# Softmax row sums: from ones-matmuls and a trip through DRAM to accumulating exponentials, with the score matmuls issued twice

## The reference

```python
def _L0_attn_ref(x, gamma, Wq, Wkv, Wo):      # 16 heads of 64, one shared key/value head
    xn = layer_norm(x, gamma)
    q = xn @ Wq
    k, v = jnp.split(kv_input @ Wkv, 2, axis=-1)
    sim = jnp.einsum('bhid,bjd->bhij', q * SCALE, k)
    sim = jnp.where(j_idx > i_idx, neg, sim)
    attn = jax.nn.softmax(sim, axis=-1)
    out = jnp.einsum('bhij,bjd->bhid', attn, v)
    return out @ Wo
def _L0_ffn_ref(x, W_fc, W_proj):
    h = jnp.square(jax.nn.relu(x @ W_fc.T))
    y = h @ W_proj.T
    ...                                        # five threshold steps on y
    return jnp.sum(spks, axis=0) / NUM_STEPS
x = x + 0.5 * _L0_ffn_ref(_layernorm(x), W_fc, W_proj)
x = x + _L0_attn_ref(_layernorm(x), gamma, Wq, Wkv, Wo)
x = x + 0.5 * _L0_ffn_ref(_layernorm(x), W_fc, W_proj)
```

## Time and profile before

| | us |
|---|---|
| median of 3 runs | 2724.68 |
| lowest and highest run | 2653.78, 2790.25 |
| the profiled execution | 2656.24 |
| its span, slowest core (core 3) | 2654.7 |
| spans of the 8 cores | 2634.5 to 2654.7 |
| mean granted TensorE clock of the cores | 0.799 to 0.812 |

### The profile page before, as it was taken

One profiled execution on the slowest core, in us unless ns is written; L12 is line 12 of the kernel. 1 busy time (PEld: TensorE's weight loads), 2 busy tenths in 40 slices (PEclk: granted clock), 3 DMA queues, 4 the chain that ended last, 5 costly groups with the idle time before them and its releaser, 6 DMA issues.

```text
span 2654.7 us, 20937 instructions; the slowest of 8 cores (2634.5 to 2654.7 us)
## 1 busy us (share of the span) xinstructions
PE 1732.8 (65%) x6660; PEld 619.3 (23%) x6660; DVE 876.8 (33%) x1482; ACT 560.6 (21%) x1004; POOL 109.0 (4%) x207
## 2 busy tenths in 40 slices
PE   0396599998355535344556655565664869999993
PEld 0042244443011101011111111111111324444441
DVE  0420364462454443232211121111112432536345
ACT  0320111030200022222323433234240221202010
POOL 1001000002200000000000000000001000000000
PEclk9897899999689655666677676676767979999997
DMA  9509312203610121322334334434435102231322
GB/s 218 107 32 232 101 56 80 96 33 103 95 23 14 15 48 32 72 48 55 64 72 75 60 73 80 77 64 79 87 64 152 70 17 77 74 131 55 132 72 80
DMA packets 320380, 206.86 MB, mean 78 GB/s; under 512 B 289914, under 2 KB 294074, under 8 KB 307986
## 3 DMA queue, kind: packets, MB, share of 16 engines
q1 hardware_dynamic: 293442, 104.22, 18.6%
q0 software_dynamic: 25680, 92.92, 13.3%
q10 hardware_dynamic: 1152, 8.39, 1.0%
HBM read 125.82 MB, written 25.38 MB: 57 GB/s over the span
## 4 chain that ended last, share of the span: by engine, by line
PE 52%; DMA 18%; DVE 14%; ACT 6%; issue 5%; another core or an unknown queue 3%; DVEq 1%; POOL 0%; SPq 0%; ACTq 0%; POOLq 0%
PE pb L469 15%; PE pb L415 12%; PE pb L683 9%; DMA WB<-WB 8%; PE pb L690 8%; ACT WB L787 5%; DVE acc L363 4%; DMA sums_d<-acc 3%; PE pb L568 2%; PE pb L829 2%; DMA Q<-wprojT 2%; DVE acc L704 2%; DVE WB L731 2%; DMA WB<-sums_d 1%
## 5 line engine op out<-in xcount | busy, mean ns | idle before, releaser
L415 PE MATMUL pb<-Q,WB 128*128 128x512 bf16 x2048 | 457.1, 384 | 73.2 <-DVE Q L391 50.3
L787 ACT ACTIVATE WB<-pb,ncb 128x512 bf16<-128x512 f32 (+3 forms) x640 | 342.9, 650 | 715.5 <-PE pb L767 415.3
L469 PE MATMUL pb<-HB,Q 128*128 128x512 bf16 x2048 | 449.9, 382 | 47.7 <-DMA Q<-wprojT 32.6
L421 ACT ACTIVATE Q<-pb 128x512 bf16<-128x512 f32 x256 | 152.8, 597 | 747.4 <-PE pb L415 662.2
L762 PE MATMUL pb<-WB,Q 64*128 64x512 bf16 (+3 forms) x320 | 145.6, 477 | 249.1 <-ACT WB L787 249.0
L683 PE MATMUL pb<-WB 128*64 128x512 bf16 x544 | 262.3, 482 | 68.7 <-DMA WB<-WB 66.4
L415 PEld LDWEIGHTS pb<-Q,WB 128*128 128x128 bf16 x2048 | 199.2, 98 | 329.9 <-issue 101.6
L469 PEld LDWEIGHTS pb<-HB,Q 128*128 128x128 bf16 x2048 | 200.5, 98 | 297.1 <-issue 62.4
L690 PE MATMUL pb<-WB,ones 128*1 128x512 bf16 x544 | 241.1, 443 | 0.0
L704 DVE COPY acc<-pb 1x512 f32<-1x512 f32 x64 | 44.0, 687 | 418.1 <-PE pb L690 414.2
L775 DVE TENSOR_TENSOR pb<-pb,tri 128x128 f32<-128x128 f32 x256 | 76.7, 300 | 277.9 <-PE pb L767 262.5
(11 more groups left out here) (92 smaller groups left out, 877.7 us busy)
## 6 DMA issues: line engine op xcount, KB each, us to landing
Q<-wp POOLq DMA_DIRECT2D x56, 1024.0 KB, 5.1
X<-xin SPq DMA_DIRECT2D x8, 1024.0 KB, 38.3
WB<-wfcT POOLq DMA_DIRECT2D x8, 1024.0 KB, 47.2
Q<-wprojT POOLq DMA_DIRECT2D x32, 256.0 KB, 12.8
wp<-Q SPq DMA_DIRECT2D x8, 1024.0 KB, 8.3
wf<-WB ACTq DMA_DIRECT2D x8, 1024.0 KB, 18.2
WB<-wf POOLq DMA_DIRECT2D x8, 1024.0 KB, 15.9
xout<-X SPq DMA_DIRECT2D x32, 256.0 KB, 2.3
```

Of the source, the lines that this page charges most:

```text
L415: P.emit("T", lambda E, par=par, dc=dc, fc=fc: E.matmul(PB[par][:], wfc_t(dc, fc), xn_t(dc)[:], start=(dc == 0), stop=(dc == DC - 1)), inc ...
L421: P.emit("A", lambda E, par=par: E.activation(hh_t(par)[:], PB[par][:], AF.Relu), inc=("a_rl", 1))
L469: st=st, sp=sp: E.matmul(PB[dc][:], wpe_t(par, fcl, dc), h_t(fc), start=st, stop=sp), inc=mark)
L787: b=(bA, bB)[hl], pc=pc: E.activation(p2_t(par, pc, hl, N), PB[b][:, 0:N], AF.Exp, bias=ncb[:, pc:pc + 1], scale=1.0),
```

## The change

It has four parts.

- **Sums.** The 544 matmuls with ones (L690) and bank `obs` go. Each exponential also adds up its row (`accum_out`) into a column of `sacc`, which VectorE clears for each query tile (new L710; the tile's first exponential waits for that).
- **`emit_msc`.** VectorE reduces the sums over the key blocks to 128x16 and takes their reciprocal, TensorE turns them into rows with 8 float32 transposes (2x128 each) into the free pair of score banks, VectorE copies them, TensorE spreads them with `e2`, VectorE copies the result to SBUF and multiplies as before. `sums_d`, both DMAs and the two reciprocals of 128x512 go.
- **Its place.** It is put off by a unit (`pend_msc`): it stands behind the scores of the second unit of the next query tile, and ahead of the AV step there. Where a query tile has one unit (`qt` 0 to 3), it stands ahead of the next scores.
- **Scores.** Each pair of score matmuls is issued twice, with the same operands and target.
- **Statistics "a".** They go the way of f1 and f2 (casts on VectorE, no `sgate`, banks 6 and 7), and stand ahead of the weight loads in the program; of the loads, Wq now comes before Wk and Wv. The identity matrix is loaded into `acc` after the projections.

```diff
-    def ln_stats(tag, with_t2, xwait=None, sgate=None, banks=(6, 7)):
+    def ln_stats(tag, with_t2, xwait=None):
...
     def attention():
+        ln_stats("a", with_t2=True)
...
-        P.wait("T", "v_sp", vspL + 2)
-        ln_stats("a", with_t2=True,
-                 sgate=("v_sp", lambda tb, dc: vsp_base + tb * DC + dc + 1),
-                 banks=(0, 1))
...
             if jb == 0:
-                P.wait("T", "v_msc", max(0, 2 * qt))
-                P.wait("T", "v_mc", max(0, 2 * qt))
+                P.wait("T", "v_msc", max(0, 2 * (qt - 1)))
...
-                        c = (half * 2 + hl) * 32
-                        P.emit("T", lambda E, rhs=rhs, c=c, obs=obs,
-                               st=st, sp=sp: E.matmul(
-                                   PB[obs][c:c + 1, 0:512],
-                                   ones[:, 1:2], rhs,
...
         def emit_msc(qt):
+            spb = 2 * (1 - (P.val("t_s") // 2) % 2)
+            P.wait("V", "a_ex", ex_done[qt])
+            po = (qt % 2) * 64
+            P.emit("V", lambda E, po=po: E.tensor_reduce(
+                rs16[:], sacc[:, po:po + 64].rearrange("p (g j) -> p g j", j=4),
+                axis=mybir.AxisListType.X, op=ALU.add))
+            P.drain("V")
+            P.emit("V", lambda E: E.reciprocal(rs16[:], rs16[:]),
+                   inc=("v_rs", 1))
+            P.drain("V")
+            P.wait("T", "v_rs", qt + 1)
+            P.wait("T", "a_ex")
+            for pc in range(NP):
+                P.emit("T", lambda E, pc=pc, mb=spb: E.transpose(
+                    PB[mb + pc // 4][0:2, (pc % 4) * 128:(pc % 4) * 128 + 128],
+                    rs16[:, pc * 2: pc * 2 + 2], ident),
+                    inc=("t_mst", 1) if pc == NP - 1 else None)
+            P.wait("V", "t_mst", qt + 1)
...
+            P.wait("T", "v_r2", qt + 1)
...
+            P.wait("V", "t_msm", qt + 1)
+            for half in range(2):
+                P.emit("V", lambda E, half=half, mb=spb: E.tensor_copy(
+                    msc_t(half * 512, 512), PB[mb + half][:, 0:512]))
+                P.drain("V")
+            P.emit("V", lambda E: E.engine_nop(), inc=("v_mc", 1))
...
                     P.wait("T", "a_ex", max(0, P.val("a_ex") - 2))
+                    P.wait("T", "v_mc")
+                    for rep in range(2):
...
                                p2_t(par, pc, hl, N), PB[b][:, 0:N],
-                                   AF.Exp, bias=ncb[:, pc:pc + 1], scale=1.0),
+                                   AF.Exp, bias=ncb[:, pc:pc + 1], scale=1.0,
+                                   accum_out=sacc[:, po + g * 4 + jb:
+                                                  po + g * 4 + jb + 1]),
...
                 tr_done[u] = P.val("s_tr")
+                if pend_msc is not None:
+                    emit_msc(pend_msc)
+                    pend_msc = None
```

More of the change, by code:

```diff
@@ L223, in ln_stats @@
             for dc in range(DC):
+                par = dc % 2
                 k = tb * DC + dc
[L225 to L247, removed]
                 P.wait("V", "t_sx", max(0, P.val("t_sx") - 1))
@@ L489, in attention @@
         P.wait("G", "s_wf16", 16 * DC)
+        for dc in range(DC):
+            P.emit("G", lambda E, dc=dc: E.dma_start(
+                out=WB[:, WQP + dc * 1024: WQP + dc * 1024 + 1024],
+                in_=wq[dc * 128:(dc + 1) * 128, :]), inc=("g_wq", 16))
         for dc in range(DC):
@@ L589, in attention @@
                 P.drain("V")
+        P.wait("S", "v_apa")
+        P.emit("S", lambda E: E.dma_start(out=ident, in_=identd), inc=("s_tri", 16))
         P.wait("S", "v_vt")
@@ L720, in emit_msc @@
-            P.wait("T", "g_ms2", 16 * (qt + 1))
-            P.wait("T", "v_sc", qt + 1)
-            for half in range(2):
-                P.emit("T", lambda E, half=half, obs=obs: E.matmul(
-                    PB[obs + half][:, 0:512], e2[:], r2_t(half * 512, 512),
-                    start=True, stop=True, skip_group_check=True),
-                    inc=("t_msm", 1) if half else None)
-            P.wait("V", "t_msm", qt + 1)
-            def recip_msc(E, half, obs):
-                with nc.allow_low_precision(reason="elementwise 1/s tile"):
-                    return E.reciprocal(msc_t(half * 512, 512),
-                                        PB[obs + half][:, 0:512])
@@ L733, in emit_msc @@
-            for half in range(2):
-                P.emit("V", lambda E, half=half, obs=obs:
-                       recip_msc(E, half, obs), inc=("v_mc", 1))
-                P.drain("V")
+            spb = 2 * (1 - (P.val("t_s") // 2) % 2)
[4 more added lines that the diff above has]
+                axis=mybir.AxisListType.X, op=ALU.add))
@@ new lines, in emit_msc @@
+            P.wait("V", "t_mst", qt + 1)
+            P.emit("V", lambda E, mb=spb: E.tensor_copy(
+                r2_t(0, 512), PB[mb][0:2, 0:512]))
+            P.drain("V")
+            P.emit("V", lambda E, mb=spb: E.tensor_copy(
+                r2_t(512, 512), PB[mb + 1][0:2, 0:512]), inc=("v_r2", 1))
+            P.wait("T", "v_r2", qt + 1)
+            for half in range(2):
+                P.emit("T", lambda E, half=half, mb=spb: E.matmul(
+                    PB[mb + half][:, 0:512], e2[:], r2_t(half * 512, 512),
+                    start=True, stop=True), inc=("t_msm", 1) if half else None)
@@ L737, in emit_msc @@
+            P.wait("V", "t_msm", qt + 1)
+            for half in range(2):
+                P.emit("V", lambda E, half=half, mb=spb: E.tensor_copy(
+                    msc_t(half * 512, 512), PB[mb + half][:, 0:512]))
+                P.drain("V")
+            P.emit("V", lambda E: E.engine_nop(), inc=("v_mc", 1))
+            P.wait("V", "t_av", unit_of[(qt, ((qt + 1) * 128 + 511) // 512 - 1)] + 1)
             for half in range(2):
@@ L782, in attention @@
                     P.wait("A", "t_s")
+                    if jb == 0 and pc == 0:
+                        P.wait("A", "v_sz")
                     if u >= 2 and pc == 0:
```

98 lines of the change are left out of this document (39 added, 59 removed).

## The result

The changed kernel takes 2263.2 us (median of 10 runs, 2233.76 to 2374.13) against 2653.68 us (median of 10) before. The ratio is 0.846, 95% interval 0.841 to 0.851: 15.4% faster. The profiled execution took 2242.66 us, its slowest core 2241.1 (core 6); the one before had 2654.7 (core 3).

What follows compares the result with a forecast made beforehand. The prediction took the attention loop (1079 us), with TensorE holding 52% of the chain of waits, as the bound. AV -182, other gaps +29, division -90, lead-in +3, tail -14, statistics +1: -253 from 2656 gives 2403 us, range 2270 to 2590.

Steps and rivals of the forecast that it cites:

- the 172 us: Attention loop, first AV to last AV: forecast 836 us, measured 664 us; this is the miss.
- the step that failed: AV steps without ones-matmuls: 0.45 us per AV matmul, 245 us in all, a gain of 182 us.
- side by side: Rival: AV matmuls of the two column halves overlap, so 245 us becomes 122 and the time 2281 us; chance 0.22.
- cheaper transposes: Division's float32 transposes at 0.13 us each instead of 0.43: 36 us more gain, below the range's end.
- Division: Gaps between AV steps that hold a division: 6.2 us behind the last exponential, 302 us in all, a gain of 90.
- Other gaps: The 24 gaps between AV steps without a division: 289 us in all, 29 us lost.
- Clock: Granted TensorE clock in the attention loop: above 0.66, with some AV steps starting warm.
- Lead-in, tail, statistics: Around the loop: first scores 3 us lost, last AV to output projection 14 gained, statistics "a" 1 lost.
- Cold and dear: Rival: AV always at the lower clock and the accumulation at 0.36 us per exponential, 2535 us; chance 0.13.
- Doubled scores bound the loop: Rival: repeated score matmuls overlap nothing, a pair takes 2.1 us, 2669 us, so no change; chance 0.08.
- The accumulation stops ScalarE: Rival: reading out sums drains ScalarE; 0.72 us extra per exponential cancels the gain, 0.9 gives 2749 us; chance 0.10.

Runs made afterwards that it cites:

- run 1: The kernel before without its ones-matmuls from query tile 2 on (row sums left out there), all other steps kept: 2362.2 us, ratio 0.889.
- run 2: The kernel before with the same matmuls reordered, in each AV step all AV matmuls first, then all ones-matmuls: 2395.4 us, ratio 0.902.
- run 3: The kernel before with a 128x64 block of ones replacing the ones column, still in turns; sum copies, both DMAs and `e2` matmuls go: 2241.3 us, ratio 0.848.
- run 4: The changed kernel with each AV step issuing all matmuls of the first column half, then all of the second: 2265.1 us in the profiled run, no ratio.
- run 7: The changed kernel with plain exponentials, row sums left out and `sacc` filled with ones: 2204.3 us, ratio 0.830 to the kernel before.

## Why the prediction was wrong where it was

**AV, 123 of the 172 us: the step that failed.** The prediction said "What stays is 0.34 us per AV matmul at the upper clock and 0.57 at the lower, weight load included" and took 0.45. These are the rows of the alternating order, and the price was a property of that order: runs 1 to 3 show the same matmul at half of 0.43 us once its neighbours have its width. Over the loop the 544 came to 122 us, 0.22 each. The rival "side by side" had the right mechanism and cited the rule that fits, and was given 0.22. What was said against it, a weight load in the open between an AV and a ones-matmul, was itself a symptom: it was in the open because of the change of width. Had the rival been taken, 2281 would have been the time, 18 above the median and 38 above the profiled execution. That its 122 us are the measured ones is in part luck: it halved 0.45, a mix of both clocks with the load in the open, where the steps ran with the load hidden and nearly all at the lower clock (0.52 granted within them, 0.77 before).

**The range.** It ended at 2270, at "side by side", although the prediction itself named 36 us more below that, for cheaper transposes. Rival and cheap transposes together, 2245, would have covered the measured 2263; the range left the combination out.

**Which half of the gain was the ones-matmuls' own.** Forecast 182 us; AV fell by 308. Run 1 got most of it without touching the division.

**Division, 39 us.** The mechanism was right, the terms too dear. Eight float32 transposes take 1.88 us, not 3.4 (0.23 each, between the 0.13 below and the 0.43 taken); copies and `e2` matmuls were right to 0.2 us (0.68, 0.69, 1.00 in the chain); between them stand 0.4 us of semaphores, forecast 0.3. Together 4.7 instead of 6.2. The other term is the accumulation: forecast at 0.22 per exponential, it came to 0.095, which is 2.0 us less over the 16 of a full unit. By size these two make 3.5 us in a gap with a plain second unit, and there 3.1 were seen: 17 us, forecast 20.

**Other gaps, 10 us.** 279 against 289: plain ones stayed at 11.8 behind the transpose, as forecast; short ones went to 10.3 to 10.9, forecast 11.4, since the accumulation is cheaper.

**Clock.** The prediction expected more than 0.66 and some AV steps that start warm. It fell to 0.60, and in run 1, where AV's busy time went too, to 0.55. That was the wrong way round in the forecast and cost AV its warm steps, yet two matmuls in 0.43 us are still cheaper than one in 0.34.

**Lead-in, tail, statistics.** From the first score to the first AV 23.6 to 26.7, +3.0 (forecast 3). Tail 23.1 to 13.8, 9.3 gained (forecast 14): Wo's load took 13.3 us behind 3.3 us of issue, and AV and division run beside it as said; but that AV step was 3.6 us and not the 7.2 of the forecast, so that more of the load stands behind it. Statistics: from the last spike of f1 to their last copy 29.4 us before and 31.1 after, +1.7 (forecast 1). The last copy, in VectorE's timeline, answering to the earlier trace rows:

```profile
730.70 0.68 DVE L237 COPY stg<-pb 1x512 f32<-1x512 f32 x1
```

**The rivals.** "Cold and dear" had the clock nearly right and both prices wrong. "Doubled scores bound the loop" fell: a pair's repeat costs latency, 25 us in all, and not throughput. "The accumulation stops ScalarE" fell: 0.095 us against the 0.72 at which the whole gain would have been gone.

## What to carry to other kernels

Before pricing what stays when an instruction goes, ask what its rows owed to the neighbour: matmuls that use a part of the array's columns run side by side while all have one width, and a narrow one between them costs far more than itself. Where a narrow matmul is needed, group it behind the wide ones of the unit (10% here, for an order), or widen it to their width. Issuing matmuls twice raised the granted clock in all three kernels here and made none of them measurably faster: where a DMA or ScalarE ends a gap, the clock helps only what TensorE does between the gaps, and the repeat can lengthen the gap.

## What the runs showed of the hardware that was not expected

- A change between 64-column and one-column weights: 16 pairs in turns take 12.2 us, the same in two blocks 5.46 all at the lower clock (run 2), and 32 in turns that all have 64 columns 5.3 at both clocks (run 3).
- Weight loads of 128x64 are hidden behind running matmuls of the same 128 rows, in the same column half too: 0.43 us a matmul at the lower clock (run 4).
- One-column matmuls in four column strips run four side by side: 16 in 1.83 us at the lower clock (run 2).
- Matmuls of the second column half seem to run beside the first half's although they stand four instructions behind them in the program: in run 4 two matmuls come in one slot from 1588.37 on, the fifth, when the first half has four of its eight matmuls to go.
- A row sum from the accumulator: an ACTIVATION_READ_ACCUMULATOR of 0.20 us, of which 0.095 us shows per exponential of 128x512 (run 7).
- Doubling the scores moved the granted clock of the loop from 0.66 to 0.71 and 0.72 in two kernels and from 0.56 to 0.60 in a third, and removing the ones-matmuls moved it from 0.66 to 0.55.
